# Decoder stage 1: the gated recurrence scanned with a ratio of clamped products, and rotated queries summed in the score matmuls

## The reference

```python
# block-diagonal gates of x, then a recurrence over the positions
gate_x = sigmoid(block_diag(x, w_in, b_in)); gate_a = sigmoid(block_diag(x, w_a, b_a))
a = exp(-(softplus(-a_param) + ... ) * gate_a)               # a decay in (0, 1), at most 1 - 1e-5
xs = sqrt(1 - a*a) * gate_x * x
p = maximum(concat([1], cumprod(a)[:-1]), 1e-7)              # clamped prefix product
h = p * cumsum((xs + 1e-7) / p)
x1 = layernorm(x + h)
# rotary (xpos) attention to ctx without softmax, a decay mask in place of it
q = xpos(x1 @ Wq, scale); k = xpos(ctx @ Wk, 1/scale); v = ctx @ Wv
x2 = layernorm(x1 + (decay * (q k^T)) v)
# then a mixture of experts, and a second layer
```

## Time and profile before

| what | value |
|---|---|
| time, median of three runs | 1986.97 us (1985.8 to 1987.6) |
| span of the profiled execution | 1985.3 us |
| phase A in it | 0 to 372 us |
| TensorE busy in the span | 1628.2 us (82%) |
| VectorE busy | 1343.2 us (68%) |
| ScalarE busy | 796.2 us (40%) |
| GpSimd busy | 512.6 us (26%) |

### The profile page before, as it was taken

How to read it: one execution, slowest core, us unless ns; L and a number is a source line. 1 busy time by engine, 2 the same in 40 slices (tenths; PEclk the granted TensorE clock), 3 DMA queues, 4 the chain that set the end, 5 groups by cost and what they waited for, 6 DMA issues and landing times.

```text
span 1985.3 us, 33988 instructions
## 1 busy us (share of the span) xinstructions
PE 1628.2 (82%) x12405; PEld 1409.1 (71%) x12405; DVE 1343.2 (68%) x2571; ACT 796.2 (40%) x1383; POOL 512.6 (26%) x584
## 2 busy tenths in 40 slices
PE   4667776674999999967777788898959999898997
PEld 3556665464988888965656566676738888888897
DVE  4889999610555555527888779998976566564664
ACT  3334444121444444522333356565623333333332
POOL 1223232175000000015555210101103333333333
PEclk8888988697999999988999889999979999999999
DMA  5331100485022223111222132111000000000000
GB/s 163 117 117 33 48 32 26 149 279 198 4 101 95 95 100 102 47 55 50 82 64 67 66 128 65 44 65 66 33 27 8 16 22 14 21 22 12 22 12 17
DMA packets 98408, 133.32 MB, mean 67 GB/s; under 512 B 8499, under 2 KB 83485, under 8 KB 97766
## 3 DMA queue, kind: packets, MB, share of 16 engines
q1 hardware_dynamic: 87526, 106.68, 16.1%
q0 software_dynamic: 6144, 16.41, 2.5%
q10 hardware_dynamic: 4608, 8.39, 1.1%
HBM read 81.50 MB, written 50.33 MB: 66 GB/s over the span
## 4 chain that ended last, share of the span: by engine, by line
PE 24%; DVE 12%; issue 12%; POOL 4%; ACT 3%; DVEq 0%; POOLq 0%; DMA 0%; ACTq 0%
PE psum L495 11%; POOL d_g_parts L1867 2%; PE psum L1617 2%; PE psum L1604 2%; DVE arena_x L1714 2%; PE psum L1307 1%; DVE arena_y L446 1%; DVE arena_x L1722 1%; DVE arena_y L1425 1%; PE psum L1593 1%; DVE arena_x L1716 1%; PE psum L460 1%; PE psum L468 1%; PE psum L476 1%; PE psum L1583 1%
## 5 line engine op out<-in xcount | busy, mean ns | idle before, releaser
L1867 POOL TENSOR_TENSOR d_g_parts<-arena_x,d_g_parts 128x512 fp32r<-128x512 f32 x128 | 164.5, 1285 | 315.8 <-ACT d_g_parts L1957 315.8
L495 PE MATMUL psum<-d_x_parts,d_v_high 128*128 128x256 f32 x1024 | 200.6, 294 | 30.6 <-DVE arena_x L2073 24.1
L495 PE MATMUL psum<-d_v_high,d_g_parts 128*128 128x256 f32 x1024 | 208.5, 286 | 13.1 <-POOL d_g_parts L1867 13.1
L495 PEld LDWEIGHTS psum<-d_x_parts,d_v_high 128*128 128x128 f32 x1024 | 161.7, 195 | 41.4 <-DVE arena_x L2073 27.6
L2073 DVE SCALAR_TENSOR_TENSOR arena_x<-arena_x,psum 128x512 f32<-128x512 f32 x128 | 87.8, 686 | 150.5 <-ACT arena_x L1965 150.2
L495 PE MATMUL psum<-m_w_high,m_h_parts 128*128 128x256 f32 x1024 | 188.0, 284 | 0.0
L495 PEld LDWEIGHTS psum<-d_v_high,d_g_parts 128*128 128x128 f32 x1024 | 170.2, 193 | 16.4 <-POOL d_g_parts L1867 16.4
L1137 ACT ACTIVATE arena_x<-psum,b_e 128x512 f32<-128x512 f32 x128 | 88.2, 689 | 196.0 <-PE psum L495 94.0
L495 PE MATMUL psum<-m_xF_parts,m_w_high 128*128 128x512 f32 x512 | 159.3, 393 | 2.1 <-DVE m_xF_parts L490 2.1
L495 PEld LDWEIGHTS psum<-m_w_high,m_h_parts 128*128 128x128 f32 x1024 | 160.7, 192 | 0.0
L1965 ACT ACTIVATE arena_x<-psum 128x512 f32<-128x512 f32 x128 | 76.4, 597 | 183.5 <-PE psum L495 183.5
(11 more groups left out here) (261 smaller groups left out, 3964.3 us busy)
## 6 DMA issues: line engine op xcount, KB each, us to landing
arena_y<-in_L_ffn_w SPq DMA_DIRECT2D x16, 1024.0 KB, 7.9
arena_x<-x_d SPq DMA_DIRECT2D x48, 256.0 KB, 2.8
arena_x<-in_ctx SPq DMA_DIRECT2D x32, 256.0 KB, 4.0
disp_d<-zeros ACTq DMA_DIRECT2D x32, 256.0 KB, 2.7
x_d<-arena_x SPq DMA_DIRECT2D x32, 256.0 KB, 2.1
kv_d<-arena_x SPq DMA_DIRECT2D x16, 512.0 KB, 3.6
arena_x<-disp_d SPq DMA_DIRECT2D x16, 512.0 KB, 8.8
y_d<-arena_x SPq DMA_DIRECT2D x16, 512.0 KB, 9.3
```

What stands on the lines that cost most here:

```text
L495: ins = nc.tensor.matmul(dst, left[a_], right[b_], start=start and k == 0, stop=stop and k == 2, skip_group_check=True)
L1867: nc.gpsimd.tensor_tensor(K["gP"][:, s % 2, 1], K["g"][:, s % 2], K["gP"][:, s % 2, 0].bitcast(F32), ALU.subtract).then_inc(d_gl, 1)
```

## The change

The recurrence is rewritten. With u = min-clamped product of 1/a (each capped at 1, reset to 1e-7 at the start of a sequence), the ratio of consecutive clamped prefix products is r = max(a, u), and h obeys h = r * h_before + (xs + 1e-7), which one scan does. So:

- VectorE no longer makes the shifted copy of a, 1 - a*a, the reciprocal, the input product and its division. It clamps 1/a (`inv`), scans `u`, takes `r = max(a, u)`, adds 1e-7, and scans `h`.
- The gate product and the scan of `u` of u0 now stand ahead of r2 of u2 in VectorE's order; r and the rotation products of Q follow r2's statistics.
- ScalarE gets two more exp (1/a, on 2 x 127 of 256 columns each) and a Square ahead of the square root.
- GpSimd's product is now m * g (ahead of VectorE's last scan) in place of p * sum (behind it); r1 = h + x stays behind the scan.
- The products of the rotation with sin are one operation over 512 columns instead of two over 256, the sign is in the table. For queries the two products are kept, not summed, and the scores sum them: 16 matmuls for 8.
- The rotation of Q moves ahead of x2 of u2. r2 and the masked scores move to another part of SBUF.

```diff
@@ a_tensor
                 if u2:
-                    done(pe, a_qr, u2)
+                    done(pe, a_qp, u2, 2)
                     done(pe, a_kr, u2)
                     done(pe, a_lg, u2.back(2))
                     for b in range(UB):
                         for c in range(NC_):
-                            ins = nc.tensor.matmul(bank(7)[:, b * S:(b + 1) * S],
-                                                   A["kr"][:, u2.p, c, b * S:(b + 1) * S],
-                                                   A["qr"][:, u2.p, c, b * S:(b + 1) * S],
-                                                   start=(c == 0), stop=(c == NC_ - 1))
+                            for kind in range(2):
+                                ins = nc.tensor.matmul(bank(7)[:, b * S:(b + 1) * S],
+                                                       A["kr"][:, u2.p, c, b * S:(b + 1) * S],
+                                                       A["qp"][:, u2.p, kind, c ^ kind, b * S:(b + 1) * S],
+                                                       start=(c == kind == 0), stop=(c == kind == 1))
                     ins.then_inc(a_score, 1)
@@ a_scalar
                     ins.then_inc(a_dec, 1)
+                    done(act, a_u, u0.back(2))
+                    for c in range(NC_):
+                        ins = nc.scalar.activation(seq(A["inv"][:, u0.p, c, :])[:, :, 1:S],
+                                                   seq(A["tha"][:, u0.p, c, :])[:, :, 0:S - 1], ACT.Exp,
+                                                   bias=pdecay[:, c:c + 1], scale=pdecay[:, c:c + 1])
+                    ins.then_inc(a_inv, 1)
...
                 if u0:
-                    done(act, a_m2, u0)
-                    nc.scalar.activation(A["m"][:, u0.p], A["m"][:, u0.p], ACT.Sqrt).then_inc(a_rt, 1)
+                    done(act, a_min, u0)
+                    done(act, a_mg, u0.back(2))
+                    nc.scalar.activation(A["m"][:, u0.p], A["a"][:, u0.p], ACT.Square, scale=0.5).then_inc(a_sq, 1)
+                    done(act, a_sq, u0)
+                    nc.scalar.activation(A["m"][:, u0.p], A["m"][:, u0.p], ACT.Sqrt, bias=0.25,
+                                         scale=-1.0).then_inc(a_rt, 1)
@@ a_vector
                 if u0:
                     done(dve, a_dec, u0)
-                    done(dve, a_thx, u0)
-                    nc.vector.tensor_scalar(sh4[:, :, 1:S], a4[:, :, 0:S - 1], 1.0 - A_EPS, None,
-                                            ALU.min).then_inc(a_sh, 1)
-                    done(dve, a_sh, u0)
                     nc.vector.tensor_scalar(A["a"][:, p], A["a"][:, p], 1.0 - A_EPS, None, ALU.min).then_inc(a_min, 1)
+                    done(dve, a_inv, u0)
+                    nc.vector.tensor_scalar(A["inv"][:, p], A["inv"][:, p], 1.0 / (1.0 - A_EPS), None,
+                                            ALU.max).then_inc(a_cap, 1)
                 if u1:
                     done(dve, aT_x1, u1.back(2))
                     done(dve, a_r2, u1.back(2))
                     ln_apply(dve, u1, seqs(bank(4)), A["x1"][:, u1.p], A_st1, ln1)
+                if u0:
+                    done(dve, a_thx, u0)
+                    done(dve, a_mg, u0.back(2))
+                    nc.vector.scalar_tensor_tensor(A["g"][:, p], A["thx"][:, p], 1.0, A["xF"][:, p], ALU.add,
+                                                   ALU.mult).then_inc(a_g1, 1)
+                    done(dve, a_cap, u0)
+                    nc.vector.tensor_tensor_scan(flat["u"], flat["inv"], table("cap"), 1.0, ALU.mult,
+                                                 ALU.min).then_inc(a_u, 1)
                 if u2:
                     done(dve, a_ret, u2)
                     done(dve, a_x2, u2.back(1))
...
                     ln_stats(dve, u2, A["r2"], A_st2, ln2)
                 if u0:
...
+                    done(dve, a_u, u0)
                     done(dve, a_min, u0)
+                    nc.vector.tensor_tensor(quads(A["r"])[:, :, 1:S], quads(A["a"][:, p])[:, :, 0:S - 1],
+                                            quads(A["u"])[:, :, 0:S - 1], ALU.max).then_inc(a_r, 1)
+                if u1:
+                    done(dve, a_q, u1)
+                    done(dve, a_score, u1.back(2))
+                    xpos(bank(4), "xpos_q_cos", "xpos_q_sin", A["qp"][:, u1.p, 0], A["qp"][:, u1.p, 1], a_qp)
...
                 if u0:
...
+                    done(dve, a_mg, u0)
+                    nc.vector.tensor_scalar(A["h"][:, p], A["h"][:, p], SCAN_EPS, None, ALU.add).then_inc(a_xe, 1)
+                    done(dve, a_xe, u0)
+                    done(dve, a_r, u0)
+                    nc.vector.tensor_tensor_scan(flat["h"], flat["r"], flat["h"], 0.0, ALU.mult,
+                                                 ALU.add).then_inc(a_h, 1)
@@ a_gpsimd
                 if u0:
-                    done(pool, a_s, u0)
-                    nc.gpsimd.tensor_tensor(A["m"][:, u0.p], A["pp"][:, u0.p], A["w"][:, u0.p],
-                                            ALU.mult).then_inc(a_h, 1)
+                    done(pool, a_rt, u0)
+                    done(pool, a_g1, u0)
+                    done(pool, a_r1, u0.back(2))
+                    nc.gpsimd.tensor_tensor(A["h"][:, u0.p], A["m"][:, u0.p], A["g"][:, u0.p],
+                                            ALU.mult).then_inc(a_mg, 1)
```

More of the change, by code:

```diff
@@ L84, in constants @@
         "ones": np.ones((P, P), f),
-        "floor": row(np.where(first, 1.0, SCAN_EPS)),
-        "keep": row(np.where(first, 0.0, 1.0)),
+        "cap": row(np.where(first, SCAN_EPS, 1.0)),
         "keep_seg": row(seg.astype(f)),
@@ L511, in decoder @@
             A[n] = arena_x.take([P, 2, UB, D])
-        for n in ("xF", "cF", "thx", "tha", "a", "ash", "m", "g", "pp", "w", "r1", "x1F", "qr", "kr", "x2F"):
+        for n in ("xF", "cF", "thx", "tha", "a", "inv", "m", "g", "h", "r1", "x1F", "kr", "x2F"):
             A[n] = arena_x.take([P, 2, NC_, T])
-        A["rp"] = arena_x.take([P, NC_, T])
+        A["qp"] = arena_x.take([P, 2, 2, NC_, T])
+        A["u"] = arena_x.take([P, NC_, T])
+        A["r"] = arena_x.take([P, NC_, T])
         A["t1"] = arena_x.take([P, NC_, T])
@@ L518, in decoder @@
             A[n] = arena_x.take([P, 2, UB, D])
-        A["r2"] = arena_x.take([P, UB, D])
-        A["sc"] = arena_x.take([P, 2, UB, S])
+        A["r2"] = arena_y.take([P, UB, D])
+        A["sc"] = arena_y.take([P, 2, UB, S])
         A_st1 = sb("A_st1", [P, UB, 10])
@@ L708, in bc, with xpos @@
                 return table(name)[:, None, :].broadcast_to([P, n, S])
-            def xpos(src, cos, sin, s_t):
-                t1, t2 = A["t1"], A["t2"]
+            def xpos(src, cos, sin, t1, t2, s_t):
                 q = src.rearrange("p (c b s) -> p c b s", c=NC_, b=UB)
[L714 to L724, removed]
+                nc.vector.tensor_tensor(t1.rearrange("p c (b s) -> p (c b) s", b=UB),
+                                        src.rearrange("p (n s) -> p n s", s=S), bc(cos, NC_ * UB),
+                                        ALU.mult).then_inc(s_t, 1)
+                turn = table(sin).rearrange("p (c s) -> p c s", c=NC_)[:, :, None, :]
+                nc.vector.tensor_tensor(t2.rearrange("p c (b s) -> p c b s", b=UB), q,
+                                        turn.broadcast_to([P, NC_, UB, S]), ALU.mult).then_inc(s_t, 1)
             def step(t):
@@ L729, in step @@
                     p = u0.p
-                    a4 = A["a"][:, p].rearrange("p c (b s) -> p (c b) s", b=UB)
-                    sh4 = A["ash"][:, p].rearrange("p c (b s) -> p (c b) s", b=UB)
-                    flat = {n: A[n][:, p].rearrange("p c t -> p (c t)") for n in ("ash", "pp", "w")}
+                    flat = {n: A[n][:, p].rearrange("p c t -> p (c t)") for n in ("inv", "h")}
+                    flat |= {n: A[n].rearrange("p c t -> p (c t)") for n in ("u", "r")}
                     done(dve, a_k, u0)
                     done(dve, a_kr, u0.back(1))
-                    done(dve, a_qr, u0.back(2))
-                    xpos(bank(5), "xpos_k_cos", "xpos_k_sin", a_kt)
+                    xpos(bank(5), "xpos_k_cos", "xpos_k_sin", A["t1"], A["t2"], a_kt)
                 if u2:
@@ L787, in step @@
                 if u0:
-                    done(dve, a_rt, u0)
-                    done(dve, a_g1, u0)
-                    nc.vector.tensor_tensor(A["g"][:, p], A["m"][:, p], A["g"][:, p], ALU.mult).then_inc(a_g2, 1)
-                    done(dve, a_g2, u0)
-                    done(dve, a_rp, u0)
-                    nc.vector.scalar_tensor_tensor(A["w"][:, p], A["g"][:, p], SCAN_EPS, A["rp"][:, :, :], ALU.add,
-                                                   ALU.mult).then_inc(a_w, 1)
-                    done(dve, a_w, u0)
-                    nc.vector.tensor_tensor_scan(flat["w"], table("keep"), flat["w"], 0.0, ALU.mult,
-                                                 ALU.add).then_inc(a_s, 1)
-                if u1:
-                    done(dve, a_q, u1)
```

(16 more changed lines are left out.)

49 lines of the change are left out of this document (22 added, 27 removed).

## The result

The changed kernel takes 2038.93 us (median of 4 runs, 2037.01 to 2040.79) for 1986.38 before, a ratio of 1.0262, 95% interval 1.0248 to 1.0276: slower by 52.5 us. Forecast was 2030.0. The span of the profiled execution is 2037.4, 52.1 more. Phase A ends, with the last copy of routing logits, at 430.8 for 371.9. So phase A costs 59.0 more; the later phases, whose instructions are the same, took 6.9 less in this execution, which no part of the change explains. There the same 11252 matmuls kept TensorE busy for 8.0 us less, at a granted clock of 0.95 for 0.94.

A forecast was written before the change was run, and what follows sets the result against it. TensorE's own round was taken to bound most steps, not VectorE's work. Terms 24.1 + 11.6 + 7.8 - 4.0 + 7.2 - 4.0 + 0.3 = 43.0 on a span of 1985.3 gave a median of 2030.0 us, range 2012 to 2045.

The forecast's parts named there:

- The scan ahead of r2: VectorE's gate product and scan now precede r2, so TensorE's V starts 1.85 us later each step: 24.1 us over 13 steps.
- Scores: 8 more score matmuls in TensorE's round, 0.89 us a step: 11.6 us over 13 steps.
- Square: New ScalarE activation between logits copy and table load, in front of K, 0.6 us a step: 7.8 us.
- the extra-load rival: Square brings its own ScalarE table load in front of K, 1.28 us each: 18 us, 2048; chance 0.06.
- L724's waits: TensorE's waits for VectorE's last queue operation, the half sum of Q, in four of 13 steps, disappear: -4.0 us.
- Clock: TensorE at 1.2 GHz after its two idle spells costs 3.2 us a step for 2.65: 7.2 us over 13 steps.
- Head and end: Outside the 13 steps: steps 0 to 2 gain 4.0 us, step 15 up to the last r1 loses 0.3.
- V does not wait for the scan: Rival: only scores and Square lengthen TensorE's round, +10 us, 1997; chance 0.08.
- VectorE's queue held the step: Rival: VectorE's queue was what held the step, so the change is faster, 1962; chance 0.06.

The follow-up runs named there:

- e1: The changed kernel with VectorE's r2 and its statistics back ahead of the gate product and the scan of u: 1994.3 us, ratio 1.0047 to the kernel before.
- e4: The kernel before with only VectorE's order changed, the gate product and the two operations of 1 - a*a ahead of r2: 2023.2 us, ratio 1.0203.
- e2: The changed kernel with a query's two rotation products summed again by VectorE, and 8 score matmuls for 16: 2031.7 us, ratio 1.0249.
- e10: e9 with the queries summed by VectorE and 8 score matmuls: 1923.9 us, ratio 0.9687 to the kernel before.
- e3: The changed kernel with ScalarE's Square moved from behind the logits copy to ahead of the x1 copy: 2020.1 us, ratio 1.0181.
- e7: The changed kernel with unused matmuls each step, 12 ahead of the wait for x1 and 7 ahead of V's wait for r2: 2011.6 us, ratio 1.0127.
- e5: The changed kernel with ScalarE's Square, table load and square root ahead of the x1 copy: 1988.8 us, ratio 1.0006.
- e8: The changed kernel with VectorE's rotation of Q behind x2 of u2 again, as before: 2032.7 us, ratio 1.0235.
- e6: The changed kernel with the 32 DMA issues that zero a buffer in steps 2 to 5 on SyncE instead of ScalarE: 2009.4 us, ratio 1.0113.
- e12: The kernel before with ScalarE's root ahead of the copy of V and the zeroing DMAs on SyncE: 1967.1 us, ratio 0.9889.
- e9: The changed kernel with r2 ahead of gate product and scan, Square and root ahead of the x1 copy, zeroing DMAs on SyncE: 1921.2 us, ratio 0.9667.

## Why the prediction was right, point by point

Direction and mechanism held. In the sum the clock's term was too small, and two costs stood at nothing: the longer DMA issues and the scores of the last step. The 13 steps grew by 59.6 us where the sum had 46.7. That the median lies inside the range owes something to luck: with later phases as long as before, it would have been 1986.4 + 59.0 = 2045.4, at the range's upper end of 2045.

- *The scan ahead of r2*, forecast 24.1: 2.31 - 0.60 = 1.71 a step, 22.2. Shown by e1 and, apart from the rest of the change, by e4. The scan took 1.13 from start to start there, not 1.25.
- *Scores*, 11.6: 5.74 - 4.94 = 0.80, 10.4. e2's phase A agrees in sign, e10 shows that the price depends on what else is late.
- *Square*, 7.8: 4.38 - 3.84 = 0.54, 7.0. e3. One table load each before tanh and root: the extra-load rival is out.
- *L724's waits*, -4.0: gone, as forecast.
- *Clock*, 7.2: this is the mis-sized term. A steady round in the kernel after is 5.74 + 2.31 + 1.83 + 1.73 + 4.38 + 2.27 + 1.73 = 19.99 at the upper clock, and 23.88 was measured: 3.89 lost a step, 4.6 to 4.75 in steps 3 to 5. I let each of two spells cost 1.7 at most; but V loses 1.75 and then Q 0.46 more, and K with the transposes 1.03 and the gates 0.65. Over 13 steps what remains of the 59.6 is 18.6 (59.6 - 22.2 - 10.4 - 7.0 + 4.0 - 5.4), above my bound of 13. e7 shows the cause for V and Q, and e5, where K and the gates are fast in every steady step, for those two. e1, e3 and e5 say the same from the other side: each took away a wait (1.71, 0.54 and 2.12 us a step, 14 times) and gained 1.9, 2.5 and 1.7 times as much as that wait. The Trainium skill (TensorE: Matmul & The Clock Gate, Part 1: The HAM clock gate) says that the throttled clock is the default; the estimate of 3.4 a step by that was nearer than my 3.2 and still too low.
- *Not in the forecast*: ScalarE's 8 DMA issues grew to 6.3 us in steps 3 and 4 and 5.94 in step 5 (4.83, 4.80 and 4.04 before), since x2, and with it SyncE's three issues, moved relative to them: logits to K 10.51, 10.49 and 10.22 for 8.32, 8.29 and 7.61, less 0.54 each, 5.4 us. I had counted DMA issues as a fixed cost of the ScalarE queue. e8, which gives back 5.5 us of phase A, and e6 show that it is no fixed cost.
- *Head and end*: the scores of step 2 start 3.28 earlier (forecast 4.0); from those of step 15 to the last logits it is 46.0 for 43.3, +2.7, forecast +0.3. The last r1 came 8.2 behind the logits, near the 8.5 of the forecast; what the sum lacked, 2.4, stands behind it, 1.75 of it in the last run of scores: 16 at the lower clock take 3.43 us to the next matmuls, where 8 at the upper clock took 1.68.
- Together -3.3 + 59.6 + 2.7 = 59.0 for phase A, where the forecast had 43.0. The later phases gave 6.9 back, so the forecast looks closer than its sum was.
- I wrote that VectorE would be idle 6 to 8 us a step; it is 13.2 (25.55 - 12.35). My own numbers already gave 11: a step of 24.6 less 18.9 - 5.5 of work. Its work fell by 6.6 a step, not 5.5, since the second half sum of Q (L724), which I had counted at 0.4, had taken 1.49 us in 15 of 16 steps; off the path, neither moved the time.

*V does not wait for the scan* fell with the L782 wait. *VectorE's queue held the step*: before the change only in four steps of 13, as read; e12 shows that it becomes the bound at 19.3 us once TensorE's waits are gone.

## What to carry to other kernels

When the busiest engine is not the one the others wait for in most steps, write down the round of the engine that is waited on, piece by piece, and ask of each moved operation which buffer it now holds longer: here two operations placed ahead of the read that frees a PSUM bank made the kernel 2.2% slower, and swapping them back with two more such moves made it 3.3% faster. Count a wait on TensorE at more than its length, because the matmuls behind it may run at half the clock: here 1.6 (e4) to 2.5 times (e3). If an idle spell can't be removed, matmuls that nobody reads can be worth 10 us in 1921.

## What the runs showed of the hardware that was not expected

- Steps lock into patterns in the clock: in the kernel after, all nine steady steps took 23.82 to 23.90 us with V at 1.2 GHz, in e3 they alternated between 21.6 and 22.7, in e9 they went 16.1, 17.7, 17.4. What decides the pattern stays open.
- DMA issues of two engines that fall together lengthen each other: eight on ScalarE 6.3 us for 4.5, and SyncE's load of ctx 1.06 for 0.50. How long depends on when they meet (4.83 in the kernel before), and one case (5.2 in step 5 of e8) has no overlap at all.
- Phases with the same instructions took 1602 to 1614 us in different kernels; in the kernel after, TensorE was busy 1368.1 us there for 1376.1 before, VectorE 1039.3 in both. The granted clock was 0.95 for 0.94; why it differed wasn't tried.
